# A four-layer block with a selective scan: elementwise steps moved from VectorE to ScalarE and GpSimd, and the router's small tiles to PSUM

## The chip, the cores and the metric

The kernel runs on one core of a Trainium2 chip. The metric is the device time of one execution in microseconds (us). Five engines work side by side, each in the order of its own instructions: TensorE (PE; its weight loads are PEld), VectorE (DVE), ScalarE (ACT), GpSimd (POOL), and SyncE (SP), which only issues DMAs here. An engine waits for another at a semaphore.

## What is computed

Eight sequences of 512 tokens with 256 channels pass through four layers; each adds its normalized output to its input:

```
x = x + layernorm(attention(layernorm(x)))   # 2 heads; q, k, v = relu(...), y = relu(attn @ v @ Wo + bo), bf16
x = x + layernorm(experts(layernorm(x)))     # 8 experts, 2 per token, and a shared one
x = x + layernorm(mamba(layernorm(x)))       # 512 inner channels, 16 states
x = x + layernorm(ternary_mlp(layernorm(x))) # 256 -> 1024 -> 256, relu squared, rms norm
```

In the experts the router's scores are `sqrt(softplus(x @ gate_w.T))`, and the two best of eight (with `gate_b`) weigh each token. In the mamba layer `delta = softplus(...)`, then for each channel and state `state = exp(delta * A) * state + delta * u * B`, `y = sum of state * C`, `y = (y + D * u) * silu(z)`, and a product with `W_out`.

## The kernel before

A sequence's tokens lie as four tiles of 128 in the 128 partitions, or, turned, its channels lie in the partitions and its 512 tokens along the free axis. The mamba layer's 512 channels are four tiles (`ct`), and each of the 16 states of each tile is one scan over 512 tokens: 64 scans (0 to 63) a sequence.

The work of a sequence is cut into four chains, lists of steps with an engine each. EARLY is the attention and the router (in PSUM bank `XE`), LATE the experts, the mamba layer's projections, its convolution and softplus, BACK the z gate, `W_out`, the MLP and the output. The scan itself is the fourth. In iteration s the scan of sequence s runs with LATE of s+1, EARLY of s+2, BACK of s-1, and the z gates of s. Before iteration 0 stands a prologue: EARLY of sequence 0 by itself, then LATE of 0 with EARLY of 1. At the end BACK of sequence 7 runs by itself. Iterations 1 to 4 are one loop body of two, run twice; the others stand in a row.

The 64 scans set the frame of an iteration. Around scan n, on 128x512 tiles: ACT makes the decay (`Exp`, L919), PE spreads B over the partitions into PSUM (L743, two buffers), DVE multiplies it by `du` (L1210), DVE scans (L1203, three `state` buffers), POOL multiplies the state by C (`prod`, L1226, four buffers), and PE sums the products of a tile's 16 states in `ps_y` (L750). After each tile's last state DVE adds `D * u` (L1216) and frees `ps_y`. SP loads C, eight scans' worth in flight at most. The other chains' steps are dealt between the scans by `in_slots`, by a table of costs for each kind of step, and each engine's order is fixed by that: a step stands behind a given scan on its engine, and whoever comes too early waits, with all that is behind it.

```
            if part == 0 and 0 <= n < PER:
                eng.wait_ge(c_spread[n % 8], s.count(2 * PER, 16 * (n // 8 + 1)))
                wait(eng, reduced, s.count(PER, n + 1 - NP))
                eng.wait_ge(scanned, s.count(PER, n + 1))
                nc.gpsimd.tensor_tensor(prod[:, n % NP, :], state[:, n % NS, :], c_all[:, n % NC, :],
                                        ALU.mult).then_inc(multiplied, 1)
```

Steps that the change touches, with their lines:

- the four norms of bf16 input: mean and variance rounded to bf16 (L942, L943), epsilon added (L946), both small, then a root on POOL (L1234) and the centring and scaling on DVE (L951, L958);
- attention, four blocks of 128 queries and two heads: the maximum (L980), its subtraction (`shift`, L984), the exponential with its sum on ACT (L781), the sum's reciprocal (L990), the multiplication by it (`probs`, L994); and the two ReLUs (L973);
- the router: scores of 128x32, comparisons on 128x256 (L997 to L1041), its root on POOL (`gate_root`, L1237). All its tiles are in SBUF;
- softplus of the mamba layer, once for each of four channel tiles: |t| and its exponential on ACT (L864, L868), (t+1)-1 (`d_round`, L1121), the difference from t (`d_fix`, L1124), the logarithm on ACT (L871), the sum (`d_sum`, L1128), all three on DVE; then `delta` (L1248) and `du` (L1252) on POOL. The log and the exponential need different tables of ACT;
- y times gate (`gated_y`, L1175) on DVE, four a sequence.

Also named: POOL's residual addition (L1270) and PE's convolution (L679) and the experts' up, weighing and down products (L619, L627, L633).

## Time and profile before

| | us |
|---|---|
| three runs | 2120.42, 2123.05, 2123.14 |
| median | 2123.05 |
| profiled execution | 2119.12 |
| its span | 2117.3 |
| prologue, to scan 0 of sequence 0 | 222.8 |
| sequence 0, from its scan 0 to that of sequence 1 | 253.4 |
| sequences 1 to 5 | 238.1, 241.6, 235.8, 235.7, 234.6 |
| sequence 6 | 208.1 |
| sequence 7, scans | 157 |
| last BACK alone | 90 |
| mean granted TensorE clock | 0.893 |

The page of the profile gives each engine's busy time over the whole span. The views of the trace used here are the busy time of each engine in stretches of time, the groups of instructions by line (busy time, mean of one, and idle time before them with what ended it), and the timeline, which lists instructions of one engine in order of time.

### The profile page before, as it was taken

To read this page: it belongs to the slowest core of one execution; us is meant where nothing else is said; L and a number is where in the kernel's file an instruction comes from. 1 tells how busy PE (TensorE), PEld (TensorE's weight loads), DVE (VectorE), ACT (ScalarE), POOL (GpSimd) and SP (SyncE) were. 2 spreads that over 40 slices of the span, in tenths; PEclk is the share of its full clock that TensorE was granted. 3 is DMA by queue.
4 is the path that set the end of the run, shared out by engine and by line. 5 is a ranking of instruction groups with operands and counts; after the bars stand their busy time and mean duration, and the time that the engine had idled before them with its cause. 6 is when DMAs were issued, how large, how long until landed. Compare 5 with 4: busy or idle time off the path is not lost. (4 is left out here: it accounts for less than half of the span.)

```text
span 2117.3 us, 22566 instructions
## 1 busy us (share of the span) xinstructions
PE 1652.8 (78%) x5874; PEld 726.1 (34%) x5948; DVE 1770.3 (84%) x3142; ACT 1035.2 (49%) x1745; POOL 918.1 (43%) x676
## 2 busy tenths in 40 slices
PE   3463566868997789968997789977997799879856
PEld 1121122323352335413352325423452335234424
DVE  6566799989979998989989998899989987987830
ACT  3247233654547355644547355554647344834322
POOL 0103324464346534464346544465346544565520
PEclk9977686979998899979998899979998899889988
DMA  3001222312222222222222222222222223223300
GB/s 107 6 1 34 80 80 65 104 65 79 71 91 84 71 77 81 88 75 71 70 95 83 72 74 80 87 76 82 70 90 84 75 80 104 90 88 116 105 20 11
DMA packets 94601, 157.95 MB, mean 75 GB/s; under 512 B 10940, under 2 KB 23660, under 8 KB 94468
## 3 DMA queue, kind: packets, MB, share of 16 engines
q1 hardware_dynamic: 94468, 156.43, 22.8%
q8 instruction: 52, 0.85, 0.2%
q14 instruction: 81, 0.66, 0.1%
HBM read 143.83 MB, written 12.58 MB: 74 GB/s over the span
## 5 line engine op out<-in xcount | busy, mean ns | idle before, releaser
L1226 POOL TENSOR_TENSOR prod<-state,c_all 128x512 f32<-128x512 f32 x512 | 675.1, 1323 | 731.4 <-DVE state L1203 665.4
L1203 DVE TENSOR_TENSOR_SCAN state<-decay,ps_b 128x512 f32<-128x512 f32 x512 | 619.3, 1209 | 9.3 <-issue 0.4
L750 PE MATMUL ps_y<-prod,idf 128*128 128x512 f32 x1024 | 617.0, 696 | 4.6 <-DVE u L1216 3.6
L1210 DVE TENSOR_TENSOR ps_b<-du,ps_b 128x512 f32<-128x512 f32 x512 | 347.4, 678 | 89.1 <-PE ps_b L743 88.8
L919 ACT ACTIVATE decay<-delta,a_neg 128x512 f32<-128x512 f32 x512 | 359.5, 719 | 36.0 <-DVE state L1203 33.0
L743 PE MATMUL ps_b<-b_rows,sel_b 48*128 48x512 bf16 x512 | 211.6, 414 | 173.8 <-DVE state L1203 169.2
L750 PEld LDWEIGHTS ps_y<-prod,idf 128*128 128x128 f32 x1024 | 186.2, 210 | 136.7 <-issue 110.4
L743 PEld LDWEIGHTS ps_b<-b_rows,sel_b 48*128 48x128 bf16 x512 | 47.8, 94 | 492.6 <-DVE state L1203 355.0
L619 PE MATMUL ps_x<-xT,w 128*128 128x512 bf16 (+1 forms) x393 | 129.8, 415 | 81.3 <-DVE arena_l L1095 71.3
L826 ACT ACTIVATE arena_l<-ps_x 128x512 f32<-128x512 f32 (+1 forms) x104 | 61.8, 594 | 194.2 <-PE ps_x L619 193.7
L535 PE MATMUL ps_x<-hT,win 128*128 128x512 bf16 (+1 forms) x456 | 136.0, 442 | 23.6 <-DVE arena_b L1171 18.7
L722 PE MATMUL ps_x<-arena_b,fcT 128*128 128x512 f32 x256 | 128.1, 624 | 6.3 <-ACT arena_b L901 4.8
L727 PE MATMUL ps_x<-pjT,arena_b 128*128 128x256 f32 x512 | 118.2, 384 | 3.1 <-ACT arena_b L907 1.7
L727 PEld LDWEIGHTS ps_x<-pjT,arena_b 128*128 128x128 f32 x512 | 95.3, 190 | 23.6 <-issue 6.4
L619 PEld LDWEIGHTS ps_x<-xT,w 128*128 128x128 bf16 (+1 forms) x416 | 32.3, 101 | 179.8 <-DVE arena_l L1095 110.5
L535 PEld LDWEIGHTS ps_x<-hT,win 128*128 128x128 bf16 (+1 forms) x480 | 48.1, 109 | 107.0 <-issue 43.1
L781 ACT ACTIVATE arena_e<-arena_e 128x512 bf16<-128x512 bf16 x64 | 39.6, 620 | 80.1 <-DVE arena_e L984 80.1
L890 ACT ACTIVATE arena_b<-ps_x 128x512 f32<-128x512 f32 x32 | 19.0, 592 | 120.8 <-PE ps_x L535 120.8
L1081 DVE SCALAR_TENSOR_TENSOR arena_l<-arena_l,ps_x 128x512 f32<-128x512 f32 (+1 forms) x104 | 69.8, 671 | 7.0 <-ACT arena_l L826 6.7
L711 PE MATMUL ps_x<-wout,u 128*128 128x256 f32 x256 | 62.1, 397 | 15.8 <-DVE u L1175 13.2
L901 ACT ACTIVATE arena_b<-ps_x 128x512 f32<-128x512 f32 x64 | 38.3, 599 | 72.5 <-PE ps_x L722 72.5
L722 PEld LDWEIGHTS ps_x<-arena_b,fcT 128*128 128x128 f32 x256 | 48.1, 197 | 63.7 <-issue 47.7
(230 smaller groups left out, 2415.7 us busy)
## 6 DMA issues: line engine op xcount, KB each, us to landing
c_all<-c_rows SPq DMA_DIRECT2D x512, 256.0 KB
c_rows<-arena_l SPq DMA_DIRECT2D x32, 256.0 KB
out<-arena_b SPq DMA_DIRECT2D x8, 512.0 KB
x_in<-in_base SPq DMA_DIRECT2D x8, 256.0 KB
c_all<-in_winT SPq DMA_DIRECT2D x1, 1280.0 KB, 7.3
arena_b<-in_w_fc SPq DMA_DIRECT2D x1, 1024.0 KB, 12.4
arena_b<-in_w_proj SPq DMA_DIRECT2D x1, 1024.0 KB, 8.3
w<-in_w1T SPq DMA_DIRECT2D x1, 792.0 KB, 5.8
```

The costliest lines, as they stand in the source:

```text
L535: ins = nc.tensor.matmul(dst, win[:, k, part, lo:lo + n], rhs[:, k, :], start=(i == 0), stop=(i == 5))
L619: ins = nc.tensor.matmul(ps_x[0:m, bank, :], w[:, k, c * P:c * P + m], xT[:, k, :], start=(k == 0), stop=(k == KD - 1))
L711: ins = nc.tensor.matmul(half_bank(XB, t), u[:, s.par, ct, t * P:(t + 1) * P], wout[:, ct, :], start=(ct == 0), stop=(ct == CT - 1))
L722: ins = nc.tensor.matmul(ps_x[:, XB, :], fcT[:, k, i * P:(i + 1) * P], x3T[:, k, :], start=(k == 0), stop=(k == KD - 1))
L727: ins = nc.tensor.matmul(ps_x[:, XB, 0:D], hf[:, m, i * P:(i + 1) * P], pjT[:, m, :], start=(m == 0), stop=(m == FM - 1))
L743: nc.tensor.matmul(ps_b[:, n % NDB, :], sel_b[lo:lo + 48, st, :].broadcast_to([48, P]), b_rows[lo:lo + 48, s.par, ct // 2, :], start=True, ...
L750: nc.tensor.matmul(ps_y[:], idf[:], prod[:, n % NP, :], start=(n % NST == 0), stop=(n % NST == NST - 1)).then_inc(reduced, 1)
L919: nc.scalar.activation(decay[:, n % NDA, :], delta[:, slot(s, ct), :], ACT.Exp, scale=a_neg[:, ct, st:st + 1]).then_inc(decayed, 1)
L1081: ins = stt(g, g, 1.0, ps_x[0:m, 0, :], ALU.add, ALU.mult)
L1203: nc.vector.tensor_tensor_scan(state[:, n % NS, :], decay[:, n % NDA, :], ps_b[:, n % NDB, :], 0.0, ALU.mult, ALU.add).then_inc(scanned, 1)
L1210: nc.vector.tensor_tensor(ps_b[:, j % NDB, :], du[:, slot(s, ct), :], ps_b[:, j % NDB, :], ALU.mult).then_inc(driven, 1)
L1226: nc.gpsimd.tensor_tensor(prod[:, n % NP, :], state[:, n % NS, :], c_all[:, n % NC, :], ALU.mult).then_inc(multiplied, 1)
```

## The change

- Attention: `shift` and `probs` are ACT's. `shift` writes max - x (scale -1, bias the maximum), and the exponential takes scale -1. The two ReLUs are ACT's.
- Norms: the roundings to bf16 and the epsilon are ACT's.
- Softplus: (t+1)-1 becomes two ACT activations (`d_one`, `d_less`), and `d_fix` and `d_sum` are POOL's.
- `gated_y` is POOL's.
- Router: seven small tiles and the 128x256 comparison tile `g_eq` move into the PSUM bank `XE`; a copy of the biased scores (`gate_twin`) is added on DVE, so that comparisons read one operand from each memory.
- The table of costs has values for the moved steps, so that steps that aren't in the diff may stand behind other scans than before.

Engines "V", "A" and "G" in the diff are VectorE, ScalarE and GpSimd.

```diff
@@ -97,7 +97,7 @@
-    r = [[("V", (site, "stats"))], [("V", (site, "aggr"))], [("V", (site, "round"))], [("V", (site, "eps16"))],
+    r = [[("V", (site, "stats"))], [("V", (site, "aggr"))], [("A", (site, "round"))], [("A", (site, "eps16"))],
@@ -128,24 +128,24 @@
-    steps = [(0, "V", "v_bias"), (1, "V", "v_relu")]
+    steps = [(0, "V", "v_bias"), (1, "A", "v_relu")]
...
-                  (b + 6, "V", ("shift", i)), (b + 7, "A", ("exp", i)), (b + 8, "V", ("sum", i)),
-                  (b + 9, "V", ("recip", i)), (b + 10, "V", ("probs", i)),
+                  (b + 6, "A", ("shift", i)), (b + 7, "A", ("exp", i)), (b + 8, "V", ("sum", i)),
+                  (b + 9, "V", ("recip", i)), (b + 10, "A", ("probs", i)),
...
-          [("V", "wo_bias")], [("V", "wo_relu")]]
+          [("V", "wo_bias")], [("A", "wo_relu")]]
@@ -176,15 +176,15 @@
-        steps += [(k, "P", ("d", i)), (k + 1, "A", ("d_abs", i)), (k + 2, "A", ("d_exp", i)), (k + 3, "A", ("d_log", i)),
-                  (k + 5, "V", ("d_sum", i)), (k + 3, "V", ("d_round", i)), (k + 4, "V", ("d_fix", i)),
-                  (k + 6, "G", ("delta", i)), (k + 7, "G", ("du", i))]
+        steps += [(k, "P", ("d", i)), (k + 1, "A", ("d_abs", i)), (k + 2, "A", ("d_exp", i)), (k + 3, "A", ("d_one", i)),
+                  (k + 4, "A", ("d_less", i)), (k + 5, "A", ("d_log", i)), (k + 5, "G", ("d_fix", i)), (k + 6, "G", ("d_sum", i)),
+                  (k + 7, "G", ("delta", i)), (k + 8, "G", ("du", i))]
...
-    r = [[("V", ("gated_y", CT - 1))]]
+    r = [[("G", ("gated_y", CT - 1))]]
@@ -208,7 +208,7 @@
-            r[-3].append(("V", ("gated_y", i - 1)))
+            r[-3].append(("G", ("gated_y", i - 1)))
@@ -230,15 +230,15 @@
-    "shift": 6, "exp": 15, "probs": 6, "turn": 8, "turned": 11, "pv": 10, "pv_out": 7, "wo": 6, "wo_out": 7,
+    "shift": 13, "exp": 15, "probs": 13, "v_relu": 10, "wo_relu": 10, "round": 4, "turn": 8, "turned": 11, "pv": 10, "pv_out": 7, "wo": 6, "wo_out": 7,
...
-    "conv": 10, "x_tanh": 8, "x_one": 7, "u": 8, "d": 10, "d_abs": 14, "d_exp": 7, "d_log": 14, "d_round": 5, "d_fix": 7,
-    "d_sum": 7, "delta": 14, "du": 14, "stats": 17, "stats0": 9, "center": 10, "divide": 10, "rstd": 10, "root": 10,
+    "conv": 10, "x_tanh": 8, "x_one": 7, "u": 8, "d": 10, "d_abs": 14, "d_exp": 7, "d_log": 14, "d_one": 7, "d_less": 7, "d_fix": 14,
+    "d_sum": 14, "delta": 14, "du": 14, "stats": 17, "stats0": 9, "center": 10, "divide": 10, "rstd": 10, "root": 10,
...
-    "gated_y": 8, "store": 8, "load": 60,
+    "gated_y": 14, "store": 8, "load": 60,
@@ -412,9 +412,8 @@
+        eps, minus = (sb(n, [P, 1]) for n in ("eps", "minus"))
@@ -426,6 +425,11 @@
+        g_q, g_c, g_s, g_tw, g_rk, cw, cwr = (
+            ps_x[:, XE, n * NT * NEXP:(n + 1) * NT * NEXP].rearrange("p (t e) -> p t e", t=NT) for n in range(1, 8))
+        g_eq = ps_x[:, XE, 256:512].rearrange("p (t i j) -> p t i j", t=NT, i=NEXP)
@@ -567,13 +571,13 @@
-                eng.wait_ge(early["V"], ea(s, "V", ("probs", i)))
+                eng.wait_ge(early["A"], ea(s, "A", ("probs", i)))
...
-                eng.wait_ge(early["V"], ea(s, "V", "v_relu"))
+                eng.wait_ge(early["A"], ea(s, "A", "v_relu"))
@@ -703,7 +707,7 @@
-                    eng.wait_ge(back["V"], bk(s, "V", ("gated_y", CT - 1)))
+                    eng.wait_ge(back["G"], bk(s, "G", ("gated_y", CT - 1)))
@@ -775,10 +779,29 @@
+            elif name == "shift":
+                eng.wait_ge(early["V"], ea(s, "V", ("max", i)))
+                for j in range(2):
+                    ins = act(ee[:, i % 2, j, :], ee[:, i % 2, j, :], ACT.Identity, bias=mx[:, i, j:j + 1], scale=-1.0)
+            elif name == "probs":
+                eng.wait_ge(early["V"], ea(s, "V", ("recip", i)))
+                for j in range(2):
+                    ins = act(ee[:, i % 2, j, :], ee[:, i % 2, j, :], ACT.Copy, scale=er[:, i, j:j + 1])
+            elif name in ("v_relu", "wo_relu"):
+                eng.wait_ge(early["V"], ea(s, "V", "v_bias" if name == "v_relu" else "wo_bias"))
+                dst = (vv if name == "v_relu" else yo).rearrange("p t d -> p (t d)")
+                ins = act(dst, dst, ACT.Relu)
+            elif i == "round":
+                eng.wait_ge(early["V"], ea(s, "V", (name, "aggr")))
+                nc.scalar.copy(mb[name][:], mv[name][:, :, 0])
+                ins = nc.scalar.copy(vb[name][:], mv[name][:, :, 1])
+            elif i == "eps16":
+                eng.wait_ge(early["A"], ea(s, "A", (name, "round")))
+                ins = act(vb[name][:], vb[name][:], ACT.Identity, bias=eps[:])
-                eng.wait_ge(early["V"], ea(s, "V", ("shift", i)))
+                eng.wait_ge(early["A"], ea(s, "A", ("shift", i)))
-                    ins = act(ee[:, i % 2, j, :], ee[:, i % 2, j, :], ACT.Exp, accum_out=es[:, i, j:j + 1])
+                    ins = act(ee[:, i % 2, j, :], ee[:, i % 2, j, :], ACT.Exp, scale=-1.0, accum_out=es[:, i, j:j + 1])
@@ -820,6 +843,7 @@
+                    wait(eng, late["G"], s.count(LPER, 0))
@@ -866,6 +890,14 @@
+            elif name == "d_one":
+                eng.wait_ge(late["A"], la(s, "A", ("d_exp", i)))
+                if i >= 2:
+                    eng.wait_ge(late["G"], la(s, "G", ("d_sum", i - 2)))
+                ins = act(d_q[:, i % 2, :], d_t(i), ACT.Identity, bias=1.0)
+            elif name == "d_less":
+                eng.wait_ge(late["A"], la(s, "A", ("d_one", i)))
+                ins = act(d_q[:, i % 2, :], d_q[:, i % 2, :], ACT.Identity, bias=minus[:])
@@ -930,21 +962,17 @@
+                elif name == "a":
+                    eng.wait_ge(early["A"], ea(s, "A", "wo_relu"))
-                    own("wo_relu" if name == "a" else ("a", "add"))
+                    own(("a", "add"))
...
-            elif i == "round":
-                own((name, "aggr"))
-                nc.vector.tensor_copy(mb[name][:], mv[name][:, :, 0])
-                ins = nc.vector.tensor_copy(vb[name][:], mv[name][:, :, 1])
-            elif i == "eps16":
-                own((name, "round"))
-                ins = ts(vb[name][:], vb[name][:], LN_EPS, None, ALU.add)
+                eng.wait_ge(early["A"], ea(s, "A", (name, "round")))
@@ -967,10 +995,6 @@
-            elif name in ("v_relu", "wo_relu"):
-                own("v_bias" if name == "v_relu" else "wo_bias")
-                dst = (vv if name == "v_relu" else yo).rearrange("p t d -> p (t d)")
-                ins = ts(dst, dst, 0.0, None, ALU.max)
@@ -978,39 +1002,34 @@
-            elif name == "shift":
-                own(("max", i))
-                for j in range(2):
-                    ins = ts(ee[:, i % 2, j, :], ee[:, i % 2, j, :], mx[:, i, j:j + 1], None, ALU.subtract)
...
-            elif name == "probs":
-                own(("recip", i))
-                for j in range(2):
-                    ins = ts(ee[:, i % 2, j, :], ee[:, i % 2, j, :], er[:, i, j:j + 1], None, ALU.mult)
...
+            elif name == "gate_twin":
+                own("gate_bias")
+                ins = nc.vector.tensor_copy(g_tw, g_bi[:])
-                own("gate_bias")
-                sj = g_bi[:].rearrange("p t (o j) -> p t o j", o=1).broadcast_to([P, NT, NEXP, NEXP])
+                own("gate_twin")
+                sj = g_tw.rearrange("p t (o j) -> p t o j", o=1).broadcast_to([P, NT, NEXP, NEXP])
@@ -1116,16 +1135,6 @@
-            elif name == "d_round":
-                eng.wait_ge(late["A"], la(s, "A", ("d_exp", i)))
-                ins = ts(d_q[:, i % 2, :], d_t(i), 1.0, -1.0, ALU.add, ALU.add)
-            elif name == "d_fix":
-                own(("d_round", i))
-                ins = tt(d_q[:, i % 2, :], d_t(i), d_q[:, i % 2, :], ALU.subtract)
-            elif name == "d_sum":
-                own(("d_fix", i))
-                eng.wait_ge(late["A"], la(s, "A", ("d_log", i)))
-                ins = tt(du[:, slot(s, i), :], du[:, slot(s, i), :], d_q[:, i % 2, :], ALU.add)
@@ -1169,10 +1178,6 @@
-            elif name == "gated_y":
-                own(("z_silu", i))
-                eng.wait_ge(y_taken, s.count(PER, NST * (i + 1)))
-                ins = tt(u[:, s.par, i, :], u[:, s.par, i, :], zs[:, i, :], ALU.mult)
@@ -1230,7 +1235,7 @@
-                eng.wait_ge(early["V"], ea(s, "V", (name, "eps16")))
+                eng.wait_ge(early["A"], ea(s, "A", (name, "eps16")))
@@ -1243,8 +1248,15 @@
+            elif name == "d_fix":
+                eng.wait_ge(late["A"], la(s, "A", ("d_less", i)))
+                ins = tt(d_q[:, i % 2, :], d_t(i), d_q[:, i % 2, :], ALU.subtract)
+            elif name == "d_sum":
+                eng.wait_ge(late["G"], la(s, "G", ("d_fix", i)))
+                eng.wait_ge(late["A"], la(s, "A", ("d_log", i)))
+                ins = tt(du[:, slot(s, i), :], du[:, slot(s, i), :], d_q[:, i % 2, :], ALU.add)
-                eng.wait_ge(late["V"], la(s, "V", ("d_sum", i)))
+                eng.wait_ge(late["G"], la(s, "G", ("d_sum", i)))
@@ -1262,6 +1274,10 @@
+            elif name == "gated_y":
+                eng.wait_ge(back["V"], bk(s, "V", ("z_silu", i)))
+                eng.wait_ge(y_taken, s.count(PER, NST * (i + 1)))
+                ins = tt(u[:, s.par, i, :], u[:, s.par, i, :], zs[:, i, :], ALU.mult)
@@ -1531,6 +1547,8 @@
+            nc.vector.memset(minus[:], -1.0)
+            nc.vector.memset(eps[:], LN_EPS)
```

Order of POOL in the iteration of sequence 5, before, from product 51 of its scan on:

```order
L1226 TENSOR_TENSOR prod<-state,c_all 128x512 x3
L1270 TENSOR_TENSOR arena_b<-arena_b 128x1024
L1226 TENSOR_TENSOR prod<-state,c_all 128x512 x2
L1237 TENSOR_TENSOR g<-g,half 128x32
L1226 TENSOR_TENSOR prod<-state,c_all 128x512
L1248 TENSOR_TENSOR delta<-du,delta 128x512
L1226 TENSOR_TENSOR prod<-state,c_all 128x512
L1252 TENSOR_TENSOR du<-delta,u 128x512
L1248 TENSOR_TENSOR delta<-du,delta 128x512
L1226 TENSOR_TENSOR prod<-state,c_all 128x512 x2
L1252 TENSOR_TENSOR du<-delta,u 128x512
```

and after, from product 53 on:

```order
L1253 TENSOR_TENSOR arena_l<-arena_l 128x512
L1231 TENSOR_TENSOR prod<-state,c_all 128x512
L1286 TENSOR_TENSOR arena_b<-arena_b 128x1024
L1231 TENSOR_TENSOR prod<-state,c_all 128x512
L1260 TENSOR_TENSOR delta<-du,delta 128x512
L1257 TENSOR_TENSOR du<-du,arena_l 128x512
L1231 TENSOR_TENSOR prod<-state,c_all 128x512
L1242 TENSOR_TENSOR g<-g,half 128x32
L1264 TENSOR_TENSOR du<-delta,u 128x512
L1260 TENSOR_TENSOR delta<-du,delta 128x512
L1253 TENSOR_TENSOR arena_l<-arena_l 128x512
L1231 TENSOR_TENSOR prod<-state,c_all 128x512 x2
```

The additions and subtractions of softplus stand between the products, and behind the router's root L1242 (L1237 before) come three more instructions before the next product, where there was none.

Order of ACT in the same iteration, before, from decay 56 on:

```order
L871 ACT_TABLE_LOAD
L871 ACTIVATE du<-arena_l 128x512
L868 ACT_TABLE_LOAD
L868 ACTIVATE arena_l<-arena_l 128x512
L798 ACTIVATE g<-ps_x 128x32
L799 ACTIVATE g<-ps_x 128x32
L517 ACTIVATE arena_b<-arena_b,sh_o,rm 128x256 x4
L919 ACTIVATE decay<-delta,a_neg 128x512
L802 ACTIVATE g<-g 128x32
L805 ACT_TABLE_LOAD
L805 ACTIVATE g<-g 128x32
L871 ACTIVATE du<-arena_l 128x512
```

and after, from decay 52 on:

```order
L951 ACTIVATE decay<-delta,a_neg 128x512
L900 ACTIVATE arena_l<-arena_l,minus 128x512
L897 ACTIVATE arena_l<-arena_l 128x512
L888 ACTIVATE arena_l<-ps_x,b 128x512
L889 ACTIVATE delta<-ps_x,b 128x512
L951 ACTIVATE decay<-delta,a_neg 128x512
L903 ACT_TABLE_LOAD
L903 ACTIVATE du<-arena_l 128x512
L900 ACTIVATE arena_l<-arena_l,minus 128x512
L892 ACT_TABLE_LOAD
L892 ACTIVATE arena_l<-arena_l 128x512
L888 ACTIVATE arena_l<-ps_x,b 128x512
```

The two activations L897 and L900 of softplus stand between the decays. Each change between the log and the exponential still costs a table load; over the whole program ACT executes 67 of them before and 77 after, two more in each of iterations 1 to 5.

Order of DVE in the same iteration, before, from scan 57 on:

```order
L1128 TENSOR_TENSOR du<-du,arena_l 128x512
L1124 TENSOR_TENSOR arena_l<-arena_l 128x512
L1203 SCALAR_TENSOR_TENSOR state<-decay,ps_b 128x512
L1210 TENSOR_TENSOR ps_b<-du,ps_b 128x512
L1128 TENSOR_TENSOR du<-du,arena_l 128x512
L1121 TENSOR_SCALAR arena_l<-arena_l 128x512
L1171 SCALAR_TENSOR_TENSOR arena_b<-arena_b,ps_x 128x512
L1203 SCALAR_TENSOR_TENSOR state<-decay,ps_b 128x512
L1210 TENSOR_TENSOR ps_b<-du,ps_b 128x512
L1175 TENSOR_TENSOR u<-u,arena_b 128x512
L1124 TENSOR_TENSOR arena_l<-arena_l 128x512
L1121 TENSOR_SCALAR arena_l<-arena_l 128x512
```

and after, from scan 56 on:

```order
L1208 SCALAR_TENSOR_TENSOR state<-decay,ps_b 128x512
L1023 TENSOR_TENSOR g<-ps_x,g 128x32
L1215 TENSOR_TENSOR ps_b<-du,ps_b 128x512
L1208 SCALAR_TENSOR_TENSOR state<-decay,ps_b 128x512
L1215 TENSOR_TENSOR ps_b<-du,ps_b 128x512
L1208 SCALAR_TENSOR_TENSOR state<-decay,ps_b 128x512
L1180 SCALAR_TENSOR_TENSOR arena_b<-arena_b,ps_x 128x512
L1215 TENSOR_TENSOR ps_b<-du,ps_b 128x512
L1208 SCALAR_TENSOR_TENSOR state<-decay,ps_b 128x512
L1215 TENSOR_TENSOR ps_b<-du,ps_b 128x512
L1026 TENSOR_TENSOR g<-g,gb 128x32
L1029 COPY ps_x<-g 128x32
```

Between two scans stood two or three of the steps of 128x512; now there is none or one, and small ones of the router.

## Rows read from the trace of the kernel before

**Rows 1.** The page, part 1: busy us, share of the span, instructions, by engine.
```profile
PE 1652.8 (78%) x5874; PEld 726.1 (34%) x5948; DVE 1770.3 (84%) x3142; ACT 1035.2 (49%) x1745; POOL 918.1 (43%) x676
```

**Rows 2.** Busy time by stretch: scans 0-15, 16-23, 24-47, 48-63 of sequence 3.
```profile
core 0: us, PE busy (x) PEld busy (x) DVE busy (x) ACT busy (x) POOL busy (x), PEclk, DMA share, GB/s
955.90:1011.00 55.10, 45.43 (x151) 19.41 (x152) 53.02 (x101) 26.22 (x46) 25.35 (x20) 0.94 0.21 72
1011.00:1038.60 27.60, 24.63 (x80) 9.39 (x80) 27.45 (x44) 16.43 (x32) 10.29 (x8) 1.00 0.24 77
1038.60:1122.70 84.10, 80.09 (x372) 44.58 (x376) 70.23 (x140) 44.75 (x79) 34.27 (x27) 1.00 0.28 88
1122.70:1191.70 69.00, 49.36 (x135) 16.91 (x136) 64.76 (x105) 40.06 (x61) 44.03 (x29) 0.78 0.21 69
```

**Rows 3.** The same view: all of sequence 0, and all of sequence 6.
```profile
222.80:476.20 253.40, 182.84 (x568) 65.74 (x578) 237.97 (x369) 113.23 (x185) 113.41 (x78) 0.78 0.23 75
1661.90:1870.00 208.10, 183.60 (x612) 80.21 (x618) 177.74 (x267) 105.54 (x171) 104.46 (x80) 0.94 0.27 88
```

**Rows 4.** Groups by line on DVE: busy us, mean ns | idle before.
```profile
L1175 DVE TENSOR_TENSOR u<-u,arena_b 128x512 f32<-128x512 f32 x32 | 35.3, 1104 | 0.3
...
L984 DVE TENSOR_SCALAR arena_e<-arena_e,mx 128x512 bf16<-128x512 bf16 x64 | 33.4, 562 | 0.2
L1121 DVE TENSOR_SCALAR arena_l<-arena_l 128x512 f32<-128x512 f32 x32 | 32.1, 1002 | 6.5 <-ACT arena_l L868 6.5
L1128 DVE TENSOR_TENSOR du<-du,arena_l 128x512 f32<-128x512 f32 x32 | 31.9, 997 | 0.0
L1124 DVE TENSOR_TENSOR arena_l<-arena_l 128x512 f32<-128x512 f32 x32 | 29.8, 930 | 0.0
...
L1016 DVE TENSOR_TENSOR x_in<-g 128x256 f32<-128x256 f32 x16 | 17.4, 1098 | 0.3
L973 DVE TENSOR_SCALAR arena_e<-arena_e 128x1024 bf16<-128x1024 bf16 x16 | 14.0, 877 | 0.1
```

**Rows 5.** Groups by line on POOL.
```profile
L1226 POOL TENSOR_TENSOR prod<-state,c_all 128x512 f32<-128x512 f32 x512 | 675.1, 1323 | 731.4 <-DVE state L1203 665.4 <-PE ps_y L750 64.6
L1248 POOL TENSOR_TENSOR delta<-du,delta 128x512 f32<-128x512 f32 x32 | 47.0, 1467 | 6.0 <-DVE du L1128 6.0
...
L1237 POOL TENSOR_TENSOR g<-g,half 128x32 f32<-128x32 f32 x8 | 43.8, 5476 | 33.9 <-DVE g L1007 33.9
L1270 POOL TENSOR_TENSOR arena_b<-arena_b 128x1024 f32<-128x1024 f32 x8 | 19.0, 2371 | 10.9 <-ACT arena_b L517 10.9
...
L1234 POOL TENSOR_TENSOR sd_y<-vb_y,hf 128x4 bf16<-128x4 bf16 x8 | 8.1, 1008 | 16.4 <-DVE vb_y L946 16.4
```

**Rows 6.** Timeline of ACT (start us, us, engine, line) at two table loads.
```profile
914.51 1.28 ACT L871 ACT_TABLE_LOAD   x1
915.80 0.63 ACT L871 ACTIVATE du<-arena_l 128x512 f32<-128x512 f32 x1
916.45 1.28 ACT L868 ACT_TABLE_LOAD   x1
```

**Rows 7.** Groups by line on PE.
```profile
L619 PE MATMUL ps_x<-xT,w 128*128 128x512 bf16 (+1 forms) x393 | 129.8, 415 | 81.3 <-DVE arena_l L1095 71.3 <-DVE arena_l L1081 3.4 <-issue 3.0
...
L679 PE MATMUL ps_x<-arena_l,wconv 128*128 128x512 f32 x64 | 34.4, 621 | 3.2 <-ACT arena_l L841 1.7 <-DVE u L1117 1.1 <-ACT arena_l L848 0.4
```

**Rows 8.** Timelines: POOL from product 48 to 63; DVE, next scan 0.
```profile
1123.85 1.28 POOL L1226 TENSOR_TENSOR prod<-state,c_all 128x512 f32<-128x512 f32 x1
...
1174.50 1.36 POOL L1226 TENSOR_TENSOR prod<-state,c_all 128x512 f32<-128x512 f32 x1 [2.09 <-DVE state L1203]
...
1183.08 1.27 POOL L1226 TENSOR_TENSOR prod<-state,c_all 128x512 f32<-128x512 f32 x1 [1.24 <-DVE state L1203]
...
1191.65 1.19 DVE L1203 TENSOR_TENSOR_SCAN state<-decay,ps_b 128x512 f32<-128x512 f32 x1
```

**Rows 9.** Timeline of DVE in the prologue, the early chain alone: one block's shift.
```profile
32.72 0.61 DVE L984 TENSOR_SCALAR arena_e<-arena_e,mx 128x512 bf16<-128x512 bf16 x2
```

26 lines of the change are left out of this document (12 added, 14 removed), and 2 rows, old and new, of the table b.

## The prediction

> **What bounds the kernel now.** I read the busy times of the whole span first [rows 1]: DVE leads with 84%, PE has 78%, ACT 49%, POOL 43%. The change takes work from DVE and gives it to the two idle engines, so a sum over DVE's busy time alone promises much. But such a share is a mean over stretches with different limits. So I cut sequence 3, an undisturbed one in the middle, at its scans and read the busy times of each stretch [rows 2]. The reader is to see three regimes. In scans 0 to 15 DVE is busy 53.0 of 55.1 us, PE 45.4: DVE binds. In scans 16 to 47 PE is busy 24.6 + 80.1 = 104.7 of 111.7 us at a granted clock of 1.00, its upper level (2.4 GHz); DVE is full for the first eight of them (27.45 of 27.60), and only 70.2 of 84.1 after. Here PE binds with some 7 us of gaps. In scans 48 to 63 and the turn to the next sequence DVE is busy 64.8 of 69.0 us, PE 49.4, ACT 40.1, POOL 44.0: DVE binds, and this is where softplus, the y times gate multiplications and the router stand. Sequence 0 has no BACK chain: DVE 238 of 253 us, PE 183 [rows 3]. In sequence 6, without EARLY, PE has 184 of 208.
>
> **The change part by part**, for such a sequence first.
>
> *Softplus and gate off DVE.* (t+1)-1, the difference and the sum cost 1.00 + 0.93 + 1.00 us and y times gate 1.10 [rows 4]; four of each are 16.1 us, all in the last stretch. The router's largest instructions there are two comparisons of 128x256 at 1.10 us [rows 4], as long as a y times gate of twice their size, so held up. What they take with one operand in PSUM is in no row; between nothing and 4.4 us (both of them and as much again of the small ones) I take 3.5 us as the gain. DVE falls from 64.8 to about 45, and no longer binds.
>
> *What POOL gets for it.* Twelve instructions of 128x512 more a sequence: with `delta` and `du` there are twenty. The order puts 19 of them between product 48 and product 63, and the last gate behind it. The bounds for one are 1.27, an undisturbed product [rows 8], and 1.47, the mean of `delta` [rows 5]. I take 1.27, since the DVE work of that size with both operands in SBUF that stood beside them is what moves away. POOL's path from the start of product 48 to the end of 63: 16 x 1.27 + 19 x 1.27 + three roots of 1.01 + addition 2.4 + router's root 5.5 [rows 5] = 20.3 + 24.1 + 10.9 = 55.3 us, where it was 20.3 + 8 x 1.27 + 10.9 = 41.4. Around it stays what is there now: scan 48 starts 1.2 us before product 48 (1122.6 and 1123.85), and from the end of product 63 (1183.08 + 1.27 = 1184.35) to scan 0 of the next sequence (1191.65) it is 7.3 us [rows 8]. The floor of the 69.0 us becomes 63.8, unless more overlaps at the turn. The order shows a block of L1242, L1264, L1260 and L1253 between two products: 5.5 + 3 x 1.27 = 9.3 us, with three state buffers; scans stop for it, but POOL itself works on, so it costs only what POOL waits for afterwards. I add 1.5 us of such waits: 65.3, a gain of 3.7 of what looked like 20. ACT has 40.1 there, and gets eight activations of 0.63 and two table loads of 1.28 more [rows 6], 7.6 us: 48 of 65, no bound.
>
> The rows show a load of 1.28 us with the activation 0.01 us behind it, twice in a row [rows 6], so the ten loads more over the program, which the order shows, are 12.8 us of ACT. The Trainium skill, "ScalarE: Activation LUTs", section "What ACT_TABLE_LOAD costs", wants a drain of about 1380 ns on top, 2.66 us for a switch; by that the ten were 26.6 us. The trace disagrees, and ACT would have room for either.
>
> *Attention.* shift and probs are 8 each of 0.56 us a sequence, the ReLUs two of 0.88 [rows 4], the roundings under 2: some 12 us of DVE. By the order most of it stood in scans 16 to 47. PE binds there, and its list changes too: three convolution products more, 3 x 2 x 0.62 = 3.7 less some overlap, 3.2, and four up products and one weighing less (0.41 each [rows 7]), -1.7, since steps moved under the new costs: PE 104.7 becomes 106.2. Of 7 us of gaps DVE's relief can close some; I take 3, so the stretch goes from 111.7 to 110.2: -1.5, between -5.5 (no gap left) and +2 (the longer chain of waits from DVE to ACT and back opens as many). Behind these costs stands cover: ACT has 61 of 111.7 busy [rows 2].
>
> *Scans 0 to 15.* The attention instructions that leave there are replaced, by the order, by steps of the experts that come earlier; the sum of DVE's work by today's durations is equal to 0.4 us. I take +0.2 us.
>
> So a full sequence gives -3.7 - 1.5 + 0.2 = -5.0; five of them (1 to 5) -25.
>
> *The other stretches.* Sequence 0 is DVE's for all its 253 us [rows 3], and what leaves DVE there counts until POOL's last stretch binds: about 12 us of attention and roundings plus half of the last stretch's gain, less what is put in its place: -11 (between 0 and -22). Sequence 6, with PE 184 of 208, -2; sequence 7 -1. The prologue gets longer: nothing runs beside the early chain there, so a step costs its own duration. A pair of shifts took 0.61 us on DVE together [rows 9], as activations two of 0.63 less overlap, 1.15: for shift and probs in four blocks 8 x 0.54 = 4.3 us, and the same again in the second chain at most, which runs beside LATE. ReLUs, roundings and softplus's steps on POOL (1.27 instead of 0.93 to 1.00, and one activation more in the chain) are some 8 more, of which half is hidden: together +11 (from +3 to +17). The end, BACK of sequence 7 alone, has none of the moved steps: 0.
>
> Sum: -25 - 11 - 3 + 11 = -28. From the profiled execution, 2119.1, that is 2091; the runs' median stands 3.9 us above it, and I say 2092, somewhat nearer the profile's own.
>
> **The rivals.**
>
> *DVE's time counts all over* (the naive sum): 8 x (16.1 + 3.5 + 12) = 253 us leave DVE, and the time would be 1866. Against it stand PE's time in the middle stretch and POOL's floor of 63.8, and I give it no chance. Its half-way form, **A**: POOL's floor is met, and products 63 and the turn overlap a bit, 62.5 instead of 69.0; the gaps of PE in the middle close (-5.5): -12 a sequence, five of them -60; sequence 0 -22, sequence 6 -6, 7 -2, prologue +5: -85, time 2034. For it: POOL stands idle 731 us before products now [rows 5] and is busy only 44 of those 69 us [rows 2], so there is room. Against it: half the moved steps wait for other engines first.
>
> **B**, slower: POOL becomes the bound with waits in it. In the last stretch it would be at 85% of 65 us, and each of its new steps waits for ACT or DVE: `d_fix` for the second activation, `d_sum` for the log behind a table load, y times gate for the gate on DVE and the y taken from PSUM behind 16 products. A product stands behind each of them, the scans behind the product (three state buffers), and all of DVE's list behind the scans. It decides from about 5.2 us of POOL's waits in these 69 us on, where the gain is spent (63.8 + 5.2). With 11 us, 75 for the stretch: +6 for each of six sequences, +36, prologue +17, and -8 for the rest: +45, time 2166. For it: POOL waits before products there even now, 2.09 us in one place [rows 8], with fewer steps between. Or POOL has no waits but its steps are longer: at 1.47 us, as `delta` [rows 5], the 35 of 128x512 take 7 us more, which leads to 72. Against both: the order gives most steps a product or more after their supplier, and the DVE steps that held POOL's up are gone. The Trainium skill, "GPSIMD Engine Reference", section "Elementwise — side-by-side cycle accounting", speaks for this rival: GpSimd takes 1.96 times as long for a two-input elementwise operation as VectorE. By that factor on the 16.1 us, POOL would get 31.6 us for them where I have 15, and the stretch would end near 80. The rows of today have 1.27 on POOL beside 0.93 to 1.10 on DVE, so the trace doesn't bear the factor out for these instructions.
>
> **C**, the change moves nothing that binds: the floors that I took from DVE are of the scan's own ring (scan, product, sum, spread), and gain and prologue cancel: within 4 us of 2123.
>
> **How the numbers follow.** Forecast 0.50 (2063 to 2108); A 0.20; B 0.17; C 0.06; small gains, 2108 to 2118, by a prologue at its upper end, 0.07. The range leaves out the outer half of A and the slow side of B: 2025 to 2148. A measurement of this kernel can tell about 0.2% (4 us) from no change. Faster by more than that: 0.50 + 0.20 + 0.07 = 0.77; within it 0.06; slower 0.17.
>
> **What the profile of the changed kernel would show.** If I am right: first scan of sequence 0 at about 234 us instead of 222.8; DVE's share near 0.72 while the time falls by 1 to 2%; scans 48 to 63 with the turn 64 to 67 us, POOL busy 57 or more of them and waits before products of a few us only; scans 16 to 47 with PE busy over 104 of 110; idle time of DVE before its scans put down to POOL's products in that stretch, where DVE has 4 us without work now. The step on scans 0 to 15 is right if they take 55 still. What would make it wrong: POOL's instructions of 128x512 at 1.47 instead of 1.27, which makes 35 of them 7 us longer and gives the whole gain back; a last stretch with POOL waiting over 5 us (B); or the middle stretch falling by 5 (A).

## The result: slower, 2158 us against 2123

The changed kernel takes 2158.3 us in the median of four runs (2157.6 to 2160.5), against 2123.1 for the kernel before: 1.0171 times as long, with a 95% interval of 1.0153 to 1.0188. The forecast was 2092 with a range of 2025 to 2148; what came is close to rival B, softplus and y times gate in POOL's row with waits, whose time was 2166. The profiled execution took 2158.4, 39.3 us over that of before.

First the page of the changed kernel, part 1, beside [rows 1]:

```profile
PE 1668.6 (77%) x5875; PEld 727.3 (34%) x5948; DVE 1566.0 (73%) x2808; ACT 1187.9 (55%) x2035; POOL 997.5 (46%) x772
```

DVE has 204 us less to do and 73% instead of 84%, as forecast, and the kernel is slower. Where the time went is read from the starts of the scans on DVE's timeline:

| us | before | after | change | forecast |
|---|---|---|---|---|
| prologue | 222.8 | 240.2 | +17.4 | +11 |
| sequence 0 | 253.4 | 246.4 | -7.0 | -11 |
| sequences 1 to 5 | 1185.8 | 1205.6 | +19.8 | -25 |
| sequence 6 | 208.1 | 215.4 | +7.3 | -2 |
| the rest | 247.3 | 248.9 | +1.6 | -1 |

Sequence 4 shows the stretches (before, it had 55.1, 111.5 and 69.0 us for scans 0 to 15, 16 to 47 and 48 to 63, like sequence 3). Busy times of the changed kernel, its scans 0 to 15, 16 to 23, 24 to 47, 48 to 63 with the turn, beside [rows 2]:

```profile
core 0: us, PE busy (x) PEld busy (x) DVE busy (x) ACT busy (x) POOL busy (x), PEclk, DMA share, GB/s
1213.30:1272.00 58.70, 44.50 (x148) 17.66 (x150) 57.34 (x99) 28.45 (x51) 25.46 (x20) 0.94 0.23 80
1272.00:1300.00 28.00, 27.84 (x119) 13.23 (x120) 23.02 (x37) 19.45 (x37) 10.18 (x8) 1.00 0.27 86
1300.00:1381.70 81.70, 80.35 (x344) 42.38 (x348) 65.66 (x125) 56.87 (x103) 33.49 (x27) 1.00 0.27 88
1381.70:1453.50 71.80, 49.34 (x124) 16.48 (x127) 43.65 (x89) 42.27 (x65) 55.14 (x41) 0.74 0.19 64
```

PE binds the middle, as said: 108.2 of 109.7 us. The first 16 scans are DVE's still, but it has 57.3 us of work there instead of 55.0: the planner has put more of the experts there. In the last stretch DVE is busy only 43.7 us of 71.8. There POOL's timeline from product 48 to product 63 is to be read, here the first, the places with idle time in brackets, and the end:

```profile
1382.98 1.28 POOL L1231 TENSOR_TENSOR prod<-state,c_all 128x512 f32<-128x512 f32 x1 [2.69 <-DVE state L1208]
...
1393.32 1.01 POOL L513 TENSOR_TENSOR rs_o<-ve_o,mhalf 128x4 f32<-128x4 f32 x1 [2.01 <-DVE ve_o L1169]
...
1396.84 1.27 POOL L1231 TENSOR_TENSOR prod<-state,c_all 128x512 f32<-128x512 f32 x1 [1.28 <-PE ps_y L754]
...
1406.34 2.35 POOL L1286 TENSOR_TENSOR arena_b<-arena_b 128x1024 f32<-128x1024 f32 x1 [4.08 <-ACT arena_b L521]
...
1444.08 1.27 POOL L1231 TENSOR_TENSOR prod<-state,c_all 128x512 f32<-128x512 f32 x1
1445.30 1.27 POOL L1264 TENSOR_TENSOR du<-delta,u 128x512 f32<-128x512 f32 x1
1446.52 1.27 POOL L1231 TENSOR_TENSOR prod<-state,c_all 128x512 f32<-128x512 f32 x1
```

and DVE's timeline at the same end:

```profile
1438.48 1.22 DVE L1208 TENSOR_TENSOR_SCAN state<-decay,ps_b 128x512 f32<-128x512 f32 x1
...
1450.03 0.75 DVE L1221 SCALAR_TENSOR_TENSOR u<-u,dpar,ps_y 128x512 f32<-128x512 f32 x1 [9.35 <-PE ps_y L754]
...
1453.50 1.19 DVE L1208 TENSOR_TENSOR_SCAN state<-decay,ps_b 128x512 f32<-128x512 f32 x1
```

From product 48 (1382.98) to the end of product 63 (1447.79) it is 64.8 us. POOL is busy for 53.9 of them and idle for 10.9: the four places above and three smaller ones, 0.43 us before L1257, 0.72 before a product and 1.04 before the router's root L1242. The forecast had 55.3 busy and 1.5 of waits. The idle time is between 10.8 and 11.0 us in each of sequences 1 to 5. In the kernel before, the same stretch of sequence 4 took 60.6 us, 42.5 busy and 18.1 idle. Scan 63 is over at 1439.70, but its product ends 8.1 us later, since products 61 and 62, two `du`, a `delta` and a gate are still to be done ahead of it, and DVE stands for 9.35 us before it can take y.

ACT's timeline shows where some of the waits begin, in the same stretch:

```profile
1385.75 0.61 ACT L897 ACTIVATE arena_l<-arena_l 128x512 f32<-128x512 f32 x1
1394.58 0.69 ACT L888 ACTIVATE arena_l<-ps_x,b 128x512 f32<-128x512 f32 x1 [8.22 <-DVE u L1221]
1395.17 0.68 ACT L889 ACTIVATE delta<-ps_x,b 128x512 f32<-128x512 f32 x1
1395.74 0.72 ACT L951 ACTIVATE decay<-delta,a_neg 128x512 f32<-128x512 f32 x1
```

L888 and L889 are softplus's first activations, and `delta` for channel tile 2 has one buffer: they wait until the y of tile 2 is taken, behind scan 51. Before, they stood behind decay 56; now they stand behind decay 52. ACT stands for 8.2 us, with the next decays, the norm of the output (for which POOL's L1286 waits) and the router's exponential queued behind. Over the whole program, groups by line on ACT and DVE (busy us, mean ns | idle before, what ended it):

```profile
L888 ACT ACTIVATE arena_l<-ps_x,b 128x512 f32<-128x512 f32 x32 | 21.8, 683 | 53.4 <-DVE u L1221 52.4 <-PE ps_x L692 0.9
...
L1208 DVE TENSOR_TENSOR_SCAN state<-decay,ps_b 128x512 f32<-128x512 f32 x512 | 620.9, 1213 | 71.2 <-ACT decay L951 30.3 <-POOL prod L1231 27.3 <-issue 0.4
...
L1013 DVE TENSOR_SCALAR ps_x<-g 128x32 f32<-128x32 f32 x8 | 1.6, 196 | 49.0 <-ACT g L825 49.0
```

Before, the scans had 9.3 us of idle time before them in all; now 71.2, of which 30.3 for decays and 27.3 for products.

### The profile page after: what moved, and what is told of

Same layout as the page of the kernel before. It is cut to its first block and busy times, and to the rows that moved or that the text cites. A ratio compares the mean times of both kernels' runs of the same rounds, so it can differ in the third digit from the quotient of the medians.

```text
span 2156.6 us, 22630 instructions
## 1 busy us (share of the span) xinstructions
PE 1668.6 (77%) x5875; PEld 727.3 (34%) x5948; DVE 1566.0 (73%) x2808; ACT 1187.9 (55%) x2035; POOL 997.5 (46%) x772
## 5 line engine op out<-in xcount | busy, mean ns | idle before, releaser
L1231 POOL TENSOR_TENSOR prod<-state,c_all 128x512 f32<-128x512 f32 x512 | 651.7, 1276 | 749.5 <-DVE state L1208 621.5
L754 PE MATMUL ps_y<-prod,idf 128*128 128x512 f32 x1024 | 634.9, 711 | 61.1 <-POOL prod L1231 55.3
L1208 DVE TENSOR_TENSOR_SCAN state<-decay,ps_b 128x512 f32<-128x512 f32 x512 | 620.9, 1213 | 71.2 <-ACT decay L951 30.3
L623 PE MATMUL ps_x<-xT,w 128*128 128x512 bf16 (+1 forms) x392 | 138.3, 438 | 80.5 <-DVE arena_l L1114 54.0
L539 PE MATMUL ps_x<-hT,win 128*128 128x512 bf16 (+1 forms) x449 | 121.2, 407 | 18.4 <-DVE arena_b L1180 10.4
L1100 DVE SCALAR_TENSOR_TENSOR arena_l<-arena_l,ps_x 128x512 f32<-128x512 f32 (+1 forms) x104 | 70.1, 674 | 13.9 <-ACT arena_l L850 13.4
L1221 DVE SCALAR_TENSOR_TENSOR u<-u,dpar,ps_y 128x512 f32<-128x512 f32 x32 | 23.7, 740 | 65.6 <-PE ps_y L754 65.6
L933 ACT ACTIVATE arena_b<-ps_x 128x512 f32<-128x512 f32 x64 | 38.2, 597 | 56.9 <-PE ps_x L726 56.8
L807 ACT COPY arena_e<-ps_x 128x1024 bf16<-128x1024 bf16 x32 | 32.6, 1018 | 61.1 <-PE ps_x L577 61.1
```

What stands on the lines that cost most here:

```text
L539: ins = nc.tensor.matmul(dst, win[:, k, part, lo:lo + n], rhs[:, k, :], start=(i == 0), stop=(i == 5))
L623: ins = nc.tensor.matmul(ps_x[0:m, bank, :], w[:, k, c * P:c * P + m], xT[:, k, :], start=(k == 0), stop=(k == KD - 1))
L754: nc.tensor.matmul(ps_y[:], idf[:], prod[:, n % NP, :], start=(n % NST == 0), stop=(n % NST == NST - 1)).then_inc(reduced, 1)
L1100: ins = stt(g, g, 1.0, ps_x[0:m, 0, :], ALU.add, ALU.mult)
L1208: nc.vector.tensor_tensor_scan(state[:, n % NS, :], decay[:, n % NDA, :], ps_b[:, n % NDB, :], 0.0, ALU.mult, ALU.add).then_inc(scanned, 1)
```

## The experiments

All were timed beside the kernel before, whose median on these chips was 2119.1 to 2122.6. The stretches are those of sequence 4; "seq 0" is the whole of sequence 0.

| kernel | prologue | seq 0 | 0-15 | 16-47 | 48-63 | median us | ratio to before (95%) |
|---|---|---|---|---|---|---|---|
| before | 222.8 | 253.4 | 55.1 | 111.5 | 69.0 | 2123 | 1 |
| changed | 240.2 | 246.4 | 58.7 | 109.7 | 71.8 | 2158 | 1.015-1.019 |
| e1, softplus on DVE | 236.8 | 235.4 | 54.2 | 109.8 | 64.2 | 2077 | 0.978-0.981 |
| e2, gate on DVE | 238.4 | 246.3 | 56.5 | 111.1 | 69.0 | 2137 | 1.007-1.010 |
| e3, both on DVE | 235.1 | 233.8 | 52.9 | 108.6 | 64.0 | 2062 | 0.972-0.975 |
| e4, both moved, no more | 229.7 | 257.3 | 60.4 | 113.1 | 75.3 | 2192 | 1.033-1.036 |
| e5, sums on DVE | 235.2 | 242.5 | 56.3 | 111.3 | 67.8 | 2133 | 1.004-1.010 |
| e6, round on DVE | 238.3 | 239.4 | 55.8 | 110.1 | 65.8 | 2114 | 0.996-0.999 |
| e7, costs of before | 234.2 | 242.2 | 57.8 | 107.5 | 70.2 | 2120 | 0.998-1.001 |
| e8, attention only | 236.9 | 243.1 | 53.0 | 107.5 | 69.2 | 2097 | 0.987-0.990 |
| e9, tiles 2, 3 later | 233.3 | 244.6 | 57.4 | 113.5 | 67.7 | 2130 | 1.003-1.007 |
| e10, router only | 221.6 | 246.1 | 55.1 | 111.5 | 65.4 | 2093 | 0.985-0.989 |
| e11, attention, router | 233.7 | 237.2 | 53.1 | 110.7 | 65.1 | 2071 | 0.973-0.978 |
| e12, e3 at old costs | 232.1 | 239.4 | 52.8 | 113.1 | 67.0 | 2089 | 0.983-0.986 |
| e13, e5 with log early | 243.9 | 239.0 | 57.2 | 110.0 | 66.3 | 2122 | 1.000-1.002 |
| e14, only sums on POOL | 239.8 | 238.3 | 54.7 | 110.5 | 64.6 | 2096 | 0.986-0.990 |
| e15, changed, mended | 241.1 | 242.0 | 59.9 | 113.0 | 66.8 | 2138 | 1.005-1.009 |

### Which part costs and which gives

**e1, softplus as before**, all else as changed; the steps' code on DVE and their costs are those of before:

```diff
-        steps += [(k, "P", ("d", i)), (k + 1, "A", ("d_abs", i)), (k + 2, "A", ("d_exp", i)), (k + 3, "A", ("d_one", i)),
-                  (k + 4, "A", ("d_less", i)), (k + 5, "A", ("d_log", i)), (k + 5, "G", ("d_fix", i)), (k + 6, "G", ("d_sum", i)),
-                  (k + 7, "G", ("delta", i)), (k + 8, "G", ("du", i))]
+        steps += [(k, "P", ("d", i)), (k + 1, "A", ("d_abs", i)), (k + 2, "A", ("d_exp", i)), (k + 3, "A", ("d_log", i)),
+                  (k + 5, "V", ("d_sum", i)), (k + 3, "V", ("d_round", i)), (k + 4, "V", ("d_fix", i)),
+                  (k + 6, "G", ("delta", i)), (k + 7, "G", ("du", i))]
```

> The changed kernel with softplus as before: (t+1)-1, the difference and the sum on DVE, no second activation; the costs of these steps as before. All else as changed. Theory (POOL's row of steps with waits between products makes the last stretch, 71.8 us for scans 48 to 63 against 69.0 before): POOL loses 8 steps of 1.27 us and the waits for ACT there, DVE gets 11.7 us back and is at about 55 of 64 busy; the stretch falls to 62 to 66 us and the kernel to about 2115 (2100 to 2130), and the prologue gets 3 us shorter. Rival (the loss is made by the attention's steps on ACT and by where the planner puts the experts' steps): the last stretch stays at 70 or more, the kernel at 2145 to 2160.

Measured 2076.8: 81 us less than the changed kernel, twice what I expected, and faster than before. The last stretch is 64.2 us as expected; the first 16 scans and sequence 0 gained 4.5 and 11 us too. The edit takes back three things at once: the engines, the rounds in which the steps stand, and their costs in the table. The runs below part them.

**e2, y times gate as before:**

```diff
-    r = [[("G", ("gated_y", CT - 1))]]
+    r = [[("V", ("gated_y", CT - 1))]]
...
-            r[-3].append(("G", ("gated_y", i - 1)))
+            r[-3].append(("V", ("gated_y", i - 1)))
```

> The changed kernel with y times gate back on DVE, at its cost of before; softplus stays on POOL and ACT. Theory (POOL's row): four steps fewer, 5.1 us, on POOL's path, of which two stand between the last products: last stretch 67 to 69, kernel about 2135 (2120 to 2145). Rival (only softplus's waits matter): last stretch within 1 us of 71.8, kernel 2150 to 2160.

Measured 2136.5, the last stretch 69.0: the first theory's numbers. From product 48 to 63 POOL is busy 51.5 us instead of 53.9 and idle 9.9 instead of 10.9.

**e3, both edits together:**

> The changed kernel with softplus and y times gate back on DVE: what is left of the change is attention, ReLUs and roundings on ACT and the router's tiles in PSUM. Theory (POOL's row): last stretch bound by DVE again, 64.8 less 3 to 4 for the router, 65 to 67 us; scans 0 to 15 at 58 if the planner's place of the experts' steps makes that, kernel 2100 to 2125. Rival (the attention on ACT is what costs): over 2145.

Measured 2062.2, less than expected and **2.7% below the kernel before: the version that beats both.** Page, part 1, then its stretches in sequence 4:

```profile
PE 1631.5 (79%) x5874; PEld 720.2 (35%) x5948; DVE 1639.7 (80%) x2936; ACT 1140.3 (55%) x1961; POOL 906.6 (44%) x676
```

```profile
1154.80:1207.70 52.90, 43.60 (x146) 17.76 (x147) 51.48 (x97) 28.47 (x52) 25.19 (x20) 0.94 0.26 90
1207.70:1231.70 24.00, 23.69 (x78) 9.17 (x78) 23.72 (x36) 18.68 (x37) 9.86 (x9) 1.00 0.26 79
1231.70:1316.30 84.60, 81.83 (x377) 45.03 (x380) 63.06 (x126) 52.73 (x95) 34.68 (x28) 1.00 0.28 90
1316.30:1380.30 64.00, 49.19 (x133) 16.95 (x134) 58.79 (x106) 40.31 (x64) 43.38 (x29) 0.79 0.22 71
```

The attention's relief shows in scans 0 to 47: 161.5 us against 166.6, with PE full in 16 to 47 (105.5 of 108.6). The last stretch, with sixteen more of the 128x512 steps on DVE than the changed kernel has, is 7.8 us shorter.

**e4, only the steps of softplus and gate moved**, on the kernel before:

> The kernel before with softplus's steps and y times gate moved as in the change, and nothing else. Theory (POOL's row): last stretch 71 to 73 us, the rest as before, prologue 3 to 5 us longer: 2140 (2130 to 2155). Rival (the attention on ACT is what costs, and DVE's relief in the last stretch is worth something): below 2115.

Measured 2191.9, 73 us over before, 52 over my figure and 37 over the upper end of its range: the move costs more than POOL's row in one stretch. In this kernel ACT stands 59.1 us at the first activation of softplus, and the first 24 scans cost 10 us more a sequence.

**e8, e10, e11: the gainful parts.** e8 is the kernel before with these lines (and the attention's code) as changed, e10 with the router's tiles as changed, e11 with both:

```diff
-                  (b + 6, "V", ("shift", i)), (b + 7, "A", ("exp", i)), (b + 8, "V", ("sum", i)),
-                  (b + 9, "V", ("recip", i)), (b + 10, "V", ("probs", i)),
+                  (b + 6, "A", ("shift", i)), (b + 7, "A", ("exp", i)), (b + 8, "V", ("sum", i)),
+                  (b + 9, "V", ("recip", i)), (b + 10, "A", ("probs", i)),
```

> The kernel before with shift and probs of the attention on ACT at their new costs, and nothing else. The attention, ReLUs, roundings and the router's tiles together gave -57 us. Theory (DVE binds in scans 0 to 23 and 48 to 63, and gaps of PE close between): -20 to -35 us, 2085 to 2100, with the prologue 5 us longer. Rival (nearly all the gain is the router's tiles): 2110 to 2120.

> The kernel before with the router's small tiles and one comparison tile in PSUM and the copy of the scores, nothing else. By my sum 3.5 us of DVE in the last stretch of each sequence: -15 to -28 us, kernel 2095 to 2108, each sequence's last stretch 65 to 66 us instead of 69. Rival (the router's chain was as late as its slowest other step, or the copy costs what it saves): within 6 us of before.

> Both, shift and probs on ACT and the router's tiles in PSUM, without ReLUs and roundings on ACT. Attention alone gave -26. If the two add up, 2075 to 2085; if ReLUs and roundings are what lifts the four together to 2062, the same; if they are worth nothing, 2058 to 2068.

Measured 2096.6, 2093.4 and 2070.7. Beside the kernel before, as it ran with each of them, the router's tiles are worth 29 us by themselves, 3.6 of them in the last stretch of sequence 4, where I had 3.5. The attention, its new costs in the table included, is worth 25 although its prologue is 14 us longer. Together they give 52, nearly the sum. The 2070.7 lie between my two figures: ReLUs and roundings add 5 to 9 us (e3; e11's runs spread from 2065 to 2079).

### Why softplus's move costs 81 us

**e5 and e6 part the two halves.** e5 has the activations on ACT but `d_fix` and `d_sum` on DVE; e6 has (t+1)-1 as one DVE instruction and those two on POOL:

```diff
-                  (k + 4, "A", ("d_less", i)), (k + 5, "A", ("d_log", i)), (k + 5, "G", ("d_fix", i)), (k + 6, "G", ("d_sum", i)),
+                  (k + 4, "A", ("d_less", i)), (k + 5, "A", ("d_log", i)), (k + 5, "V", ("d_fix", i)), (k + 6, "V", ("d_sum", i)),
```

```diff
+        steps += [(k, "P", ("d", i)), (k + 1, "A", ("d_abs", i)), (k + 2, "A", ("d_exp", i)), (k + 3, "A", ("d_log", i)),
+                  (k + 5, "G", ("d_sum", i)), (k + 3, "V", ("d_round", i)), (k + 4, "G", ("d_fix", i)),
+                  (k + 6, "G", ("delta", i)), (k + 7, "G", ("du", i))]
```

> The changed kernel with softplus's difference and sum on DVE, at their costs of before; (t+1)-1 stays as two activations on ACT, y times gate stays on POOL. It parts the two halves of softplus's move, whose sum is 2158 against 2077 without either. Theory (POOL's row): nearly all of the loss goes, scans 48 to 63 at 63 to 66 us instead of 71.8, kernel 2070 to 2100. Rival (the two activations more in ACT's row and in the chain before the log cost it): last stretch at 69 or more, kernel above 2120.

> The other half alone: (t+1)-1 is one instruction on DVE as before, without the two activations; difference and sum stay on POOL, y times gate too. Theory (POOL's row): last stretch 69 to 72, kernel 2130 to 2160. Rival (the activations cost it): 2075 to 2100.

Measured 2133.4 and 2114.3; e5's last stretch is 67.8, and e6 fits neither of its figures. My theory of POOL's row fell here as the only cause: beside e1 (2076.8) the two activations by themselves cost 57 us, the two POOL steps by themselves 37, each with its costs and rounds. The two are 94 together where both at once cost 81, so they overlap, and neither is a share of the 81. The scans' idle time tells the halves apart (e5, then e6):

```profile
L1215 DVE TENSOR_TENSOR_SCAN state<-decay,ps_b 128x512 f32<-128x512 f32 x512 | 621.1, 1213 | 12.9 <-POOL prod L1238 0.7
```

```profile
L1205 DVE TENSOR_TENSOR_SCAN state<-decay,ps_b 128x512 f32<-128x512 f32 x512 | 620.9, 1213 | 48.9 <-POOL prod L1228 36.7
```

POOL's steps make scans wait for products. ACT's don't; there DVE waits at the router instead, 45.0 us for the exponential L825 in e5 beside 18.0 in e1 and in e6, and ACT itself stands 34.3 us in e5 at softplus's first activation for PE's product L692, 9.8 in e1.

**e7, the planner's costs of before** in the changed kernel:

```diff
-    "shift": 13, "exp": 15, "probs": 13, "v_relu": 10, "wo_relu": 10, "round": 4, "turn": 8, "turned": 11, "pv": 10, "pv_out": 7, "wo": 6, "wo_out": 7,
+    "shift": 6, "exp": 15, "probs": 6, "turn": 8, "turned": 11, "pv": 10, "pv_out": 7, "wo": 6, "wo_out": 7,
...
-    "conv": 10, "x_tanh": 8, "x_one": 7, "u": 8, "d": 10, "d_abs": 14, "d_exp": 7, "d_log": 14, "d_one": 7, "d_less": 7, "d_fix": 14,
-    "d_sum": 14, "delta": 14, "du": 14, "stats": 17, "stats0": 9, "center": 10, "divide": 10, "rstd": 10, "root": 10,
+    "conv": 10, "x_tanh": 8, "x_one": 7, "u": 8, "d": 10, "d_abs": 14, "d_exp": 7, "d_log": 14, "d_one": 5, "d_less": 5, "d_fix": 7,
+    "d_sum": 7, "delta": 14, "du": 14, "stats": 17, "stats0": 9, "center": 10, "divide": 10, "rstd": 10, "root": 10,
...
-    "gated_y": 14, "store": 8, "load": 60,
+    "gated_y": 8, "store": 8, "load": 60,
```

> The changed kernel, every step on its new engine, but the planner's table has the costs of before for all of them (6 for shift and probs, 7 for the difference and the sum, 8 for y times gate, 5 for each new activation). It tells what the place of the other steps is worth. Theory: the larger costs at the end of the chain with softplus push PE's convolution into scans 16 to 23 and the experts' steps into scans 0 to 15; without them scans 0 to 23 take 80 to 83 us instead of 86.7 and the kernel 2120 to 2140. Rival (the place is worth nothing, the engines are all): within 8 us of 2158.

Measured 2120.1, with 82.7 us for scans 0 to 23, both as forecast: the table alone costs 38 us. ACT's wait for `u` before softplus's first activation is 2.7 us instead of 52.4.

**e12, the same in the good kernel:**

> Softplus and y times gate on DVE, all else as changed (the kernel at 2062), but with the planner's costs of before for shift, probs, ReLUs and roundings. It tells how much of that gain is the new place of steps in scans 16 to 47, which was 108.6 us there against 111.6 before. If the place does it: scans 16 to 47 at 111 again and 2075 or more. If the engines do: within 6 us of 2062.

Measured 2088.7 against 2062.2: here the new costs (of shift, probs, ReLUs and roundings) are worth 26 us: in sequence 4, 4.5 of them in scans 16 to 47 (113.1 against 108.6) and 3.0 behind. Read with e7, the attention's costs help, and those of softplus and the gate must be what harms, though no run has their costs alone. A table of costs is an edit of its own, with a price of either sign.

**e9, softplus of tiles 2 and 3 two rounds later**, nothing else (what I expected counts decays and scans from 1, the text here from 0):

```diff
-    d0 = (14, 15, 17, 18)
+    d0 = (14, 15, 19, 20)
```

> The changed kernel with softplus of channel tiles 2 and 3 begun two rounds later in the chain, all engines and costs as changed. In the changed kernel ACT stands 7.5 us a sequence at softplus's first activation for tile 2, which is placed behind decay 53 and waits until y of tile 2 has been taken from PSUM behind scan 52; here it stands behind decay 56. Theory (a good part of the loss is this place: ACT stands, the decays behind it come late, and the scans wait for them, 30 us over the program): ACT's wait there gone, scans' wait for decays gone, kernel 2115 to 2135. Rival (other waits take its place, POOL's row above all, since the last steps now come two rounds later too): 2145 to 2165.

Measured 2130.5, 28 us less than the changed kernel. The two groups that answer to those above:

```profile
L888 ACT ACTIVATE arena_l<-ps_x,b 128x512 f32<-128x512 f32 x32 | 21.8, 682 | 11.8 <-PE ps_x L692 11.5
...
L1208 DVE TENSOR_TENSOR_SCAN state<-decay,ps_b 128x512 f32<-128x512 f32 x512 | 621.1, 1213 | 31.4 <-POOL prod L1231 15.9 <-ACT decay L951 1.9 <-issue 0.4
```

ACT's wait for `u` is gone, and nearly all of the scans' wait for decays with it; the wait for products fell too, from 27.3 to 15.9. That this place is a cause is shown. Its 28 us are a third of the 81 in size, but like the costs of e7 they overlap with the rest: with e7's costs the same wait is nearly gone as well.

**e13, e14, e15** take the rest apart. e13 is e5, and e15 is e9, with the logarithm two rounds earlier; e14 is e6 with y times gate on DVE:

```diff
-                  (k + 4, "A", ("d_less", i)), (k + 5, "A", ("d_log", i)), (k + 5, "V", ("d_fix", i)), (k + 6, "V", ("d_sum", i)),
+                  (k + 4, "A", ("d_less", i)), (k + 3, "A", ("d_log", i)), (k + 5, "V", ("d_fix", i)), (k + 6, "V", ("d_sum", i)),
```

> As the run with the two activations on ACT and the sums on DVE (2133), but with softplus's logarithm in the round where it stood before the change, ahead of the second activation instead of behind it. The two activations cost 56 us there over 2077. If what costs is that they put off the logarithm and all behind it by two rounds: 2095 to 2115. If it is the work and the place that their costs give the other steps: within 8 us of 2133.

> Attention, ReLUs, roundings and router as changed, y times gate on DVE, softplus with one instruction for (t+1)-1 on DVE, and only the difference and the sum on POOL: the POOL half by itself beside the kernel at 2062. With y times gate on POOL too this half cost 37 us (2077 to 2114) and scans waited 37 us for products. If POOL's row is what costs, and each step in it more so the fuller it is: 2080 to 2095, scans' wait for products 15 to 25 us over the program. If POOL's steps cost by their place in the plan alone: 2095 to 2105 and the same wait as with the gate.

> The changed kernel, every step on its new engine and at its new cost, with both repairs of place: softplus of tiles 2 and 3 two rounds later (alone it gave -28), and the logarithm two rounds earlier. It tells what is left of the loss when the chain is placed well. If the two add: 2105 to 2120. If POOL's row bounds it: within 5 us of 2130.

Measured: e13 2121.9, neither of its figures (its runs spread from 2113 to 2125, so the 11 us are uncertain in size). The logarithm's place is the smaller part, and what the other 45 us of the two activations are isn't settled: ACT's wait for PE's product L692, 34.3 us in e5, is 3.5 in e13, and only 11 us of time went with it.

e14 2095.6: the two POOL steps cost 33 us beside e3 where they cost 37 with the gate there too. The scans' wait for products halves from 36.7 to 17.4, as my theory had it, but the time doesn't follow and is the rival's (2095 to 2105).

e15 2137.6, neither of its figures: the repairs don't add. Its first 16 scans take 59.9 us, and ACT stands 29.6 us for PE's product L692.

POOL's stretch from product 48 to the end of product 63 in sequence 4 tells what the last stretch followed:

| kernel | us | POOL busy | POOL idle | scans 48-63 |
|---|---|---|---|---|
| before | 60.6 | 42.5 | 18.1 | 69.0 |
| changed | 64.8 | 53.9 | 10.9 | 71.8 |
| e9 | 60.8 | 53.7 | 7.1 | 67.7 |
| e15 | 59.8 | 53.7 | 6.1 | 66.8 |
| e6 | 59.8 | 54.3 | 5.5 | 65.8 |
| e5 | 61.8 | 46.2 | 15.7 | 67.8 |
| e3 | 57.2 | 43.4 | 13.8 | 64.0 |

With all twelve steps on POOL (changed, e9, e15, e6) its work is the same 54 us, and the stretch goes by its idle time. Even the best of them has 5.5 us of it and takes 65.8, just over the forecast's 65.3. In e5, with eight steps fewer on POOL, the stretch is no shorter: there its idle time is 15.7 us, and POOL's work isn't the bound.

## Why the prediction was wrong

- **POOL's path** was the right one to sum, and its work was right: the durations of its instructions from product 48 to 63 sum to 55.4 us (55.3 forecast; 1.27 us for each step, as taken, not 1.47). Each starts some 0.04 us before the one ahead of it is over, so POOL is busy for 53.9. The step that failed is "I add 1.5 us of such waits": they measured 10.9. The longest are 4.1 before the residual addition L1286, 2.0 and 1.4 before two roots, and 1.3 for PE. That is rival B as it stood, with the 11 us that it named, past its deciding point of 5.2; what was wrong is the size that I gave the waits, and so its chance. With 1.3 us ahead of product 48 and 5.7 behind product 63 (7.3 forecast), the stretch is 1.3 + 53.9 + 10.9 + 5.7 = 71.8. The waits before the two roots could be read beforehand, from POOL's timeline of the kernel before in sequence 3:

```profile
1128.91 1.01 POOL L1267 TENSOR_TENSOR rm<-rm,mhalf 128x4 f32<-128x4 f32 x1 [3.78 <-DVE rm L1185]
...
1136.23 1.01 POOL L509 TENSOR_TENSOR rs_o<-ve_o,mhalf 128x4 f32<-128x4 f32 x1 [3.85 <-DVE ve_o L1160]
```

- **What ACT's stand explains** isn't all of these waits. A wait of that size before the residual addition stands in e1 (4.0 us), e3 (3.9) and e7 (4.4) too, where ACT waits for `u` hardly or not at all; in e9 and e15 it is gone.
- **What I didn't look for** is a wait on a buffer that the old order had kept harmless. The order of the two kernels shows softplus's first activation for tile 2 move from decay 56 to 52, and `delta`'s single buffer for tile 2 is free behind scan 51. I costed ACT by its busy time ("48 of 65, no bound") and not by where its row stands. e9 shows 28 us for it.
- **Scans 0 to 15**, "+0.2", measured +3.6. I summed the new order's rows at their old durations. The counts of the experts' steps there went from 9, 7 and 7 to 10, 8 and 8 (+2.0 us), and the bias addition of q and k (L993) took 0.99 us each instead of 0.63, four times. In e1, with softplus alone back on DVE, the counts are those of before and the stretch takes 54.2, though these bias additions still take 0.99 each; so the experts' steps come with softplus's move. e7 has 9, 8 and 7 of them and 3.1 us of idle time before the first kind (L1100), and takes 57.8.
- **The middle** came near: -1.8 measured, -1.5 forecast; but e12 shows that its time hangs on the table of costs (113.1 with the old ones), which the forecast took only into PE's list. **The router** was near too: 3.6 (e10), forecast 3.5, a choice between nothing and 4.4 and so partly luck.
- **Sequences 0 and 6** came out at -7 and +7 instead of -11 and -2. Softplus's move is in both: e1 takes 11 and 9 us off them. I didn't take them apart by stretch.
- **The prologue**: the early chain alone is 5.4 us longer in e8 (8.0 in the changed kernel), forecast 4.3 for the same steps; the second part, beside LATE, costs another 9 in e8, which I had as "the same again at most". A pair of activations took 1.33 us there, where I had 1.15. Softplus on POOL adds 3.4 (the changed kernel beside e1).
- **The rule that a GpSimd operation takes 1.96 times as long as VectorE's** (the Trainium skill, "GPSIMD Engine Reference", section "Elementwise — side-by-side cycle accounting") is nearer than I allowed. The rows of before had 0.93 to 1.10 us on DVE beside 1.27 on POOL, but these were held up; one that stood free, at 1180 us of that trace, took 0.68 us, which makes the factor 1.87. I also put the factor on the wrong sum: of the 16.1 us, (t+1)-1 goes to ACT, and POOL gets what took 12.1 on DVE, 23.7 us by that factor and not 31.6. The step itself took 1.27 us, so this rule didn't decide the time.

## What to carry to other kernels

Idle time of an in-order engine isn't room by itself. The attention's steps gained on ACT (25 us); softplus's lost, since a step that stands between two links of the loop that sets the pace can cost its own duration and the waits in front of it. Before moving work off the busiest engine, sum the row of the engine that receives it from one fixed point of the loop to the next, with a wait for each supplier on another engine, and look in the new order for every single buffer whose user now stands earlier. And time a table of planner's costs as a change by itself: here the attention's new costs were worth -26 us in one kernel, and with those of softplus and the gate among them +38 in another.

## What the hardware showed beyond that

Some operations on DVE and POOL took longer beside each other, and the router's gain is mostly that: its instructions on DVE took 69 us over the program before and 34 in e10, with a copy more, and the kernel gained 29. Before, a comparison of 128x256 took 1.10 us [rows 4]; with one operand in PSUM (changed kernel, groups by line):

```profile
L1035 DVE TENSOR_TENSOR x_in<-ps_x,g 128x256 f32<-128x256 f32 x8 | 3.2, 406 | 0.1
```

And POOL's `delta` took 1.47 us in the mean [rows 5]. With softplus's additions gone from DVE it takes 1.27; with them there and the router in PSUM (e3) it still takes 1.46:

```profile
L1260 POOL TENSOR_TENSOR delta<-du,delta 128x512 f32<-128x512 f32 x32 | 40.7, 1272 | 0.0
```

The Trainium skill, "SBUF — State Buffer", section "Who interferes with whom", says that a VectorE instruction with two SBUF inputs contends with a GpSimd instruction that reads SBUF, and one with at most one such input doesn't, unless it runs in a mode that uses two ports. The two rows agree with it. The router's first step has one input, and it too fell, from 1.21 us (L997) to 0.19 (L1001 in e10), once it wrote to PSUM; no run shows in which mode it ran.
